# Positional query columns of four heads in one product, placed by DMA copies

## The chip, the cores and the metric

The kernel runs on one core of a Trainium2 chip. A core has a matrix engine (TensorE, in the profile PE, its weight loads PEld), a vector engine (VectorE, DVE), an activation engine (ScalarE, ACT), a general engine (GpSimd, POOL) and an engine that mostly issues transfers (SyncE, SP). Each follows its own list of instructions in order, and they wait for one another by semaphores. The metric is the device time of one execution in microseconds. Before the change it is 903.84, the median of three runs (903.61 to 907.07).

## The reference

The input x is 8 batches of 512 tokens with 128 features. A modulation row per batch (silu(c) @ Wmod) gives shifts, scales and gates. The block is an attention with relative positions and a mixture of experts:

```python
h = layernorm(x) * (1 + ca) + sa
q, k, v = einsum('bsx,xAnh->Abnsh', h, w)        # 16 heads of 64
q = q + q_bias
a = einsum('bnqh,bnkh->bnqk', q, k) * 64 ** -0.5
emb = einsum('sf,fnh->nsh', sins, positional)    # 32 frequencies
pos_scores = einsum('bnqh,nvh->bnqv', q, emb) * 64 ** -0.5
a = a + relative_causal(pos_scores)              # column = distance q - k
a = softmax(where(causal, a, -1e9))
x = x + ga * (concat_heads(a @ v) @ out_kernel + out_bias)
h = layernorm(x) * (1 + cb) + sb
x = x + gb * experts(h)                          # top 1 of 16, 256 places each
```

Since the sine of a difference of positions is a sum of products, the positional score of a query and a key at distance q - k is also a product of 64 numbers made from the query (32 frequencies, each times two tables over the query's position) with 64 numbers that depend on the key's position alone. So a head's score is one product over 128 numbers: 64 of content and 64 of position.

## The kernel before, in words

There are 64 attention steps: 8 batches (b), in each 8 pairs of heads (a), j = 8b + a. Steps of even and odd a use the two halves of several buffers. A query tile `qx` holds for each of the two heads 128 partitions: 0 to 63 the content of the query, 64 to 127 its positional numbers, by 512 queries. Both come out of one product a head: the weights `whi`/`wlo` of a pair have 128 columns for each head, 64 query columns and 64 columns of a positional weight (the query weight times the positional kernel, made once at the start by `w_table`, its 32 columns stored twice), and 128 columns for the keys of both heads. Products of activations and weights are done three times, with the high and low parts of either operand (`hi*hi`, `hi*lo`, `lo*hi`), so one product is three matmuls of 512 columns. VectorE adds the bias and multiplies by the table `qtab` as it evacuates the query (`evac_q`, L1106).

Within a step the engines go through eight score groups s0 to s7 (k = 0 to 7): first the four query tiles of the first head, from 512 keys down to 128, then those of the second head. For each k:

- TensorE: the scores (L773, L770) into one of two banks, then one group of transposes of the previous step's probabilities (L783, k = 0 to 5), at k = 1 a value product (L759), at k = 2 the output projection of two steps ago (L810), after s4 the next step's query product of the first head (L738), at k = 5 the next key product (L738), at k = 7 the weighted sum of the previous step (L803), and last the next query product of the second head (L738).
- VectorE: subtracts mask and negates with a running maximum (L1089), at k = 0 one transposed group (L1097) and the low part of the attention output (L1118), at k = 1 the low part of the second head's keys (`low_k`, L1112), at k = 4 the first head's query (L1106); at the end of the step `low_k` of the next step's first head, reciprocals and the second head's query. Layer norms, gating and routing are spread over fixed (a, k).
- ScalarE: exponentials (L553), the high part of the queries (L518), transposed groups (L562), values (L522), the high part of the keys (L512) and their copy `kx` (L513), the attention output (L567). At (a, k) = (2, 4) it normalizes the next batch (`normed`, L499), out of the bank that also takes the second head's query and the value product (`prb[1]`).
- GpSimd: the low part of the queries (L388) and the division of the probabilities (L395), modulation, and the indirect writes of tokens to the experts' buffer.
- SP: weights and stores; at the start of batch 0 the gates' rows go to all partitions, the experts' buffer is filled (4 transfers) and 8 expert weights are loaded.

The order is written out by hand in the Python loops; nothing plans it. After the 64 steps comes a tail with the last batch's routing, and then the 16 experts.

## Time and profile before

| | us |
|---|---|
| median of three runs | 903.84 |
| the profiled execution's own time | 906.07 |
| its span, first to last instruction | 904.0 |
| TensorE busy | 875.8 (97%) |
| ScalarE busy | 710.3 (79%) |
| VectorE busy | 665.9 (74%) |
| GpSimd busy | 518.7 (57%) |

An engine's busy time is the time in which an instruction of it is under way. A timeline row gives the start from the start of the span, the duration, engine, line of the source, operation and tiles (what is written, then what is read). Matmuls overlap: one of 512 columns is shown with 0.40 us, but the next one starts some 0.23 us later. The distance of starts is what TensorE's order costs. The mean granted clock of TensorE is 0.991 of full speed.

### The profile page before, as it was taken

Reading aid. Unit: us, or ns where it says so; the run is one execution under the profiler, and the core shown is the slowest. Engines: PE = TensorE matmul, PEld = TensorE weight load, DVE = VectorE, ACT = ScalarE, POOL = GpSimd, SP = SyncE. Lnnn points to the kernel's source line nnn. Section 1 sums busy time; section 2 is a strip of 40 time slices with the busy share of each in tenths; the row PEclk is TensorE's granted clock in tenths of the full one; section 3 lists DMA queues with packets and bytes.
Section 4 is the critical chain, followed back from the end, with each engine's and each line's share of the span. In section 5 each row is a group of like instructions: output and inputs, shape, how many; then the busy total and the mean of one; then the engine's idle time right before and its main releaser. Section 6 shows DMA issues by size and latency. Waiting matters only on the chain.

```text
span 904.0 us, 17653 instructions
## 1 busy us (share of the span) xinstructions
PE 875.8 (97%) x5632; PEld 702.2 (78%) x5632; DVE 665.9 (74%) x2053; ACT 710.3 (79%) x1970; POOL 518.7 (57%) x786
## 2 busy tenths in 40 slices
PE   6999999999999999999999999999999999997994
PEld 5777777887777778777777877777887777766994
DVE  4778778787878687777878787868777677753884
ACT  4788888888888888888888888888888888841551
POOL 2455555565565755675557556675566556633354
PEclk9899999999999999999999999999999999999998
DMA  7000790000000000000000000000000000006671
GB/s 271 2 1 1 190 243 24 1 19 18 13 1 2 36 1 13 1 28 10 13 1 15 12 13 1 2 21 8 5 1 22 2 13 1 9 22 218 215 213 39
DMA packets 23068, 38.92 MB, mean 43 GB/s; under 512 B 3094, under 2 KB 16135, under 8 KB 22592
## 3 DMA queue, kind: packets, MB, share of 16 engines
q1 hardware_dynamic: 19184, 29.11, 11.1%
q0 software_dynamic: 3072, 5.94, 1.8%
q10 hardware_dynamic: 720, 2.75, 0.9%
q8 instruction: 45, 0.74, 0.3%
q14 instruction: 47, 0.39, 0.1%
HBM read 23.44 MB, written 16.82 MB: 45 GB/s over the span
## 4 chain that ended last, share of the span: by engine, by line
PE 86%; DVE 1%; POOL 1%; DMA 1%; issue 1%; ACT 1%; POOLq 0%; DVEq 0%
PE bank L773 21%; PE bank L803 16%; PE bank L738 15%; PE bank L783 14%; PE bank L810 5%; PE bank L759 4%; PE bank L770 3%; PE bank L981 2%; PE bank L970 2%; DMA x<-xbuf 1%; PE bank L831 1%; POOL out L443 1%; PE bank L961 0%; PE bank L818 0%; PE bank L825 0%
## 5 line engine op out<-in xcount | busy, mean ns | idle before, releaser
L395 POOL TENSOR_SCALAR prob<-prob,rsum 128x128 f32<-128x128 f32 (+3 forms) x512 | 263.1, 532 | 238.4 <-DVE rsum L1101 232.4
L553 ACT ACTIVATE prob<-srow,nmax 128x512 f32<-128x512 f32 (+3 forms) x512 | 286.3, 560 | 66.5 <-DVE nmax L1089 63.7
L1089 DVE CUSTOM_DVE_ANT_0 srow<-bank,consts 128x512 f32<-128x512 f32 (+3 forms) x512 | 247.0, 488 | 98.0 <-issue 76.4
L783 PE MATMUL bank<-consts,prob 128*128 128x128 f32 x1280 | 201.7, 272 | 0.2 <-POOL prob L395 0.2
L783 PEld LDWEIGHTS bank<-consts,prob 128*128 128x128 f32 x1280 | 158.4, 140 | 22.9 <-POOL prob L395 0.5
L388 POOL TENSOR_TENSOR qlo<-qx,qhi 128x384 fp32r<-128x384 f32 x128 | 129.5, 1012 | 54.5 <-ACT qhi L518 53.2
L562 ACT ACTIVATE pt<-bank 128x384 f32<-128x384 f32 x318 | 153.3, 495 | 5.4 <-PE bank L783 5.0
L803 PE MATMUL bank<-pt,v 128*64 128x512 f32 (+3 forms) x1024 | 152.0, 439 | 0.3 <-issue 0.2
L773 PE MATMUL bank<-khi,qhi 128*128 128x512 f32 (+2 forms) x384 | 146.0, 380 | 3.5 <-DVE klo L1112 1.7
L1106 DVE SCALAR_TENSOR_TENSOR qx<-bank,qbias,consts 128x512 f32<-128x512 f32 x128 | 94.2, 736 | 53.6 <-PE bank L738 53.5
L773 PE MATMUL bank<-khi,qlo 128*128 128x512 f32 (+2 forms) x384 | 130.4, 339 | 0.0
L773 PE MATMUL bank<-klo,qhi 128*128 128x512 f32 (+2 forms) x384 | 129.5, 337 | 0.0
L803 PEld LDWEIGHTS bank<-pt,v 128*64 128x64 f32 x1024 | 68.1, 136 | 76.8 <-issue 59.3
L1112 DVE SCALAR_TENSOR_TENSOR klo<-bank,khi 64x512 fp32r<-64x512 f32 x128 | 87.8, 686 | 18.0 <-ACT kx L513 16.0
L553 ACT ACTIVATION_READ_ACCUMULATOR prob<-srow,nmax 128x1 f32 x512 | 97.8, 191 | 0.0
L518 ACT ACTIVATE qhi<-qx 128x384 fp32r<-128x384 f32 x128 | 66.6, 521 | 37.2 <-DVE qx L1106 36.5
L773 PEld LDWEIGHTS bank<-khi,qhi 128*128 128x128 f32 x384 | 72.6, 189 | 17.0 <-issue 7.9
L738 PE MATMUL bank<-hhi,whi 128*128 128x512 f32 x177 | 81.4, 460 | 0.0
L773 PEld LDWEIGHTS bank<-klo,qhi 128*128 128x128 f32 x384 | 73.1, 190 | 7.5
L512 ACT ACTIVATE khi<-bank 64x512 fp32r<-64x512 f32 x128 | 75.2, 588 | 3.7 <-PE bank L738 2.1
L773 PEld LDWEIGHTS bank<-khi,qlo 128*128 128x128 f32 x384 | 72.5, 189 | 5.5
L738 PE MATMUL bank<-hlo,whi 128*128 128x512 f32 x177 | 70.4, 398 | 0.0
(166 smaller groups left out, 1429.4 us busy)
## 6 DMA issues: line engine op xcount, KB each, us to landing
xbuf<-fill SPq DMA_DIRECT2D x4, 1540.0 KB, 24.4
x<-xbuf SPq DMA_DIRECT2D x16, 385.0 KB, 4.0
raw<-in_w SPq DMA_DIRECT2D x16, 256.0 KB, 8.9
prob<-in_w SPq DMA_DIRECT2D x16, 256.0 KB, 4.7
out<-row SPq DMA_DIRECT2D x8, 256.0 KB, 2.3
x<-in_x SPq DMA_DIRECT2D x1, 1792.0 KB, 13.2
modb<-mod_rows SPq DMA_DIRECT2D x1, 1536.0 KB, 7.8
v<-in_b SPq DMA_DIRECT2D x1, 1024.0 KB, 7.4
```

What stands on the lines that cost most here:

```text
L388: gp.tensor_tensor(qlo[:, h, :], qx[:, h, P:S], qhi[:, h, :], ALU.subtract).then_inc(s["ql"], 1)
L395: end = gp.tensor_scalar(part, part, rsum[:, par, 4 * h + q:4 * h + q + 1], 1.0, ALU.mult, ALU.mult)
L512: act.activation(khi[0:HD, h, :], prb[0][h * HD:(h + 1) * HD, :], ACT.Copy, scale=C_QKV)
L553: act.activation(prob[:, par, h, QOFF[q]:QOFF[q] + P * (q + 1)], srow[:, k % 4, 0:P * (q + 1)], ACT.Exp, bias=nmax[:, par, k:k + 1], scale ...
L562: act.activation(pt[:, h, KOFF[g]:KOFF[g] + GW[g]], source[:, 0:GW[g]], ACT.Copy)\
L738: last = pe.matmul(out, w[:, a, cols], h, start=(i == 0), stop=(i == 2))
L773: last = pe.matmul(out, a[:, h, (q - 1) * P:q * P], b[:, h, 0:P * (q + 1)], start=(i == 0), stop=(i == 2))
L783: last = pe.transpose(out[:, n * P:(n + 1) * P], prob[:, par, h, QOFF[q] + k * P:QOFF[q] + (k + 1) * P], ident)
L803: last = pe.matmul(otb[h * HD:(h + 1) * HD, k * P:S], v[:, g, k, at + h * HD:at + (h + 1) * HD], pt[:, h, KOFF[k]:KOFF[k] + S - k * P], st ...
L1089: dve.tensor_tensor_reduce(out=srow[:, k % 4, 0:w], in0=scb[k % 2][:, 0:w], in1=mask[:, S - w:S], scale=-1.0, scalar=BIG, op0=ALU.add, op1 ...
L1106: dve.scalar_tensor_tensor(qx[:, h, :], prb[h][:, :], qbias[:, h, a:a + 1], qtab, ALU.add, ALU.mult).then_inc(s["qe"], 1)
L1112: dve.scalar_tensor_tensor(klo[0:HD, h, :], prb[0][h * HD:(h + 1) * HD, :], C_QKV, khi[0:HD, h, :], ALU.mult, ALU.subtract).then_inc(s["kl ...
```

## The change

Queries: one product a step gives the 64 content columns of both heads (128 columns). It stands ahead of s3 now, in `prb[0]`, and waits until both `low_k` of the present step have read that bank. VectorE evacuates it by two tensor_scalar of 64 partitions, ahead of s3 and s4; the second head's moves from partitions 64 to 127 of the bank to partitions 0 to 63 of `qx`.

Positional numbers: in every even step, behind s6, one product gives the 32 raw frequency columns of four heads (the next pair of steps), in `prb[1]`. VectorE evacuates it twice (`evac_g`, at k = 6 and 7), once with each of the two tables (`gtab`), into `g2`. Four transfers on SP (`spread`) then copy the parts into partitions 64 to 127 of `qx`. `qx` has two halves by the step's parity.

The value product at k = 1 waits for `evac_g` or for the tail uses of its bank. SP's order: each step's copies come first; the fill is cut into 16 transfers over the steps of batch 0, expert weights are loaded over batch 1, and the gates' rows, for two batches at a time, ahead of their use. The first step's query is still done by two products with their own weights (`fwhi`, `fwlo`), which GpSimd then copies for later batches. The weight splits are fewer and wider.

```diff
@@ SP
+            def spread(j):
+                c, odd = divmod(j, 2)
+                wait(sp, "sc", 8 * (j - 1) if j > 1 else 0)
+                sp.wait_ge(s["gq"], 2 * c + 2)
+                for h in range(2):
+                    at = odd * CH + h * FREQS
+                    for i in range(2):
+                        sp.dma_start(qx[HD + i * FREQS:HD + (i + 1) * FREQS, odd, h, :], g2[at:at + FREQS, i, :])\
+                            .then_inc(s[f"gx{odd}"], 16)
...
@@ ScalarE
             def high_q(j, h):
                 act.wait_ge(s["qe"], 2 * j + h + 1)
-                act.activation(qhi[:, h, :], qx[:, h, P:S], ACT.Copy).then_inc(s["qh"], 1)
+                wait(act, f"gx{j % 2}", 64 * ((j + 1) // 2))
+                act.activation(qhi[:, h, :], qraw(j, h)[:, P:S], ACT.Copy).then_inc(s["qh"], 1)
...
@@ TensorE
+            def project_q(j, n, a):
+                pe.wait_ge(s["kl"], 2 * j)
+                project(prb[0][:, :], whi[:, a, 0:P], wlo[:, a, 0:P], n, "qp")
+            def project_g(c):
+                project(prb[1][:, :], gwhi[:, c % NG, :], gwlo[:, c % NG, :], g_batch(c), "tp")
...
                 for k in range(8):
+                    if k == 3 and after:
...
+                        project_q(j + 1, n, m)
                     scores(j, k)
-                    if k == 4 and after:
-                        project_q(j + 1, n, m, 0)
...
                     if k == 5 and after:
...
+                        pe.wait_ge(s["qe"], 2 * j + 4)
                         project_k(j + 1, n, m)
...
+                    if k == 6 and a % 2 == 0 and j + 2 < NJ:
+                        pe.wait_ge(s["ve"], j + 4 if before else 1)
+                        if a == 2 and not last:
+                            pe.wait_ge(s["hn"], b + 2)
+                        if a == 4 and not first:
+                            pe.wait_ge(s["lge"], b)
+                        project_g(j // 2 + 1)
...
-                    project_q(j + 1, n, m, 1, 8 * B if last and V_OF[a][0] else j + 4 if before else 2)
...
@@ VectorE
             def evac_q(j, a, h):
-                dve.wait_ge(s["qp"], 2 * j + h + 1)
-                dve.scalar_tensor_tensor(qx[:, h, :], prb[h][:, :], qbias[:, h, a:a + 1], qtab,
-                                         ALU.add, ALU.mult).then_inc(s["qe"], 1)
+                dve.wait_ge(s["qp"], j + 2)
+                own = slice(h * HD, (h + 1) * HD)
+                dve.tensor_scalar(qraw(j, h)[0:HD, :], prb[0][own, :], pbias[own, a:a + 1], CQ, ALU.add, ALU.mult)\
+                    .then_inc(s["qe"], 1)
+            def evac_g(c, i):
+                dve.wait_ge(s["tp"], c + 1)
+                if c:
+                    dve.wait_ge(s["gx1"], 64 * c)
+                    wait(dve, "gx0", 64 * (c - 1))
+                dve.scalar_tensor_tensor(g2[:, i, :], prb[1][:, :], gbias[:, c % NG:c % NG + 1], gtab[:, i, :],
+                                         ALU.add, ALU.mult).then_inc(s["gq"], 1)
...
                 for k in range(8):
+                    if k in (3, 4) and after:
+                        evac_q(j + 1, (a + 1) % PAIRS, k - 3)
                     scores(j, par, k)
...
-                        if after:
-                            evac_q(j + 1, (a + 1) % PAIRS, 0)
+                    if k in (6, 7) and a % 2 == 0 and j + 2 < NJ:
+                        evac_g(j // 2 + 1, k - 6)
...
-                if after:
-                    evac_q(j + 1, (a + 1) % PAIRS, 1)
```

## Rows read from the trace of the kernel before

**Rows 1.** The page: busy time of the engines, and the chain by engine.
```profile
PE 875.8 (97%) x5632; PEld 702.2 (78%) x5632; DVE 665.9 (74%) x2053; ACT 710.3 (79%) x1970; POOL 518.7 (57%) x786
...
PE 86%; DVE 1%; POOL 1%; DMA 1%; issue 1%; ACT 1%; POOLq 0%; DVEq 0%
```
**Rows 2.** Timeline (start, duration, engine, line, names), TensorE, step (4,6) and after.
```profile
486.96 0.40 PE L773 MATMUL bank<-khi,qhi 128*128 128x512 f32 x1
...
491.04 0.38 PE L770 MATMUL bank<-kx,qx 128*128 128x128 f32 x2
...
492.43 0.40 PE L738 MATMUL bank<-hhi,whi 128*128 128x512 f32 x1
...
493.13 0.49 PE L783 MATMUL bank<-consts,prob 128*128 128x128 f32 x3
...
497.99 0.50 PE L738 MATMUL bank<-hhi,whi 128*128 128x512 f32 x1
...
498.79 0.39 PE L773 MATMUL bank<-khi,qhi 128*128 128x512 f32 x1
```
**Rows 3.** Timeline, TensorE, the first step's bias products.
```profile
23.23 1.36 PE L694 MATMUL bank<-smallT,raw 128*32 128x1 f32 x56
```
**Rows 4.** Timeline, VectorE, step (4,6).
```profile
487.95 0.69 DVE L1089 CUSTOM_DVE_ANT_0 srow<-bank,consts 128x512 f32<-128x512 f32 x1
...
490.36 0.69 DVE L1112 SCALAR_TENSOR_TENSOR klo<-bank,khi 64x512 fp32r<-64x512 f32 x1
491.08 0.42 DVE L1089 CUSTOM_DVE_ANT_0 srow<-bank,consts 128x256 f32<-128x256 f32 x1
...
492.73 0.69 DVE L1089 CUSTOM_DVE_ANT_0 srow<-bank,consts 128x512 f32<-128x512 f32 x1 [0.87 <-issue]
...
496.71 0.68 DVE L1112 SCALAR_TENSOR_TENSOR klo<-bank,khi 64x512 fp32r<-64x512 f32 x1 [0.40 <-ACT kx L513]
```
**Rows 5.** Groups by line and shape, VectorE: busy us, mean ns, idle before.
```profile
L1358 DVE TENSOR_SCALAR srow<-bank,smallT 128x256 f32<-128x256 f32 x32 | 15.2, 481 | 3.1 <-PE bank L970 2.5
...
L1128 DVE TENSOR_SCALAR hn<-bank,bo,modT 128x512 f32<-128x512 f32 x8 | 6.5, 807 | 1.2 <-PE bank L810 1.2
```
**Rows 6.** Timeline, a wait that ends: VectorE's maximum releases TensorE.
```profile
39.68 0.08 DVE L1089 DVE_READ_ACCUMULATOR2_ANT nmax<- 128x1 f32 x1
...
39.82 0.49 PE L770 MATMUL bank<-kx,qx 128*128 128x128 f32 x2 [0.67 <-DVE nmax L1089]
```
**Rows 7.** Timeline, ScalarE, step (4,6): the copy of the next keys.
```profile
496.41 0.26 ACT L513 ACTIVATE kx<-bank 64x128 f32<-64x128 f32 x1
```
**Rows 8.** Timeline, TensorE, step (4,3): transposes of the second norm.
```profile
457.14 0.60 PE L825 MATMUL bank<-consts,xh 128*128 128x128 f32 x4
```
**Rows 9.** Timeline, ScalarE and TensorE, step (4,2): the normalization, and s7.
```profile
445.23 0.77 ACT L499 ACTIVATE hn<-bank,modT 128x512 f32<-128x512 f32 x1
...
446.36 0.39 PE L770 MATMUL bank<-kx,qx 128*128 128x128 f32 x2
```
**Rows 10.** Timeline, VectorE and TensorE, step (4,4), its s0 and the next one's.
```profile
462.07 0.39 PE L773 MATMUL bank<-khi,qhi 128*128 128x512 f32 x1
...
471.65 0.42 DVE L1089 CUSTOM_DVE_ANT_0 srow<-bank,consts 128x256 f32<-128x256 f32 x1 [0.15 <-ACT prob L553]
...
473.98 0.67 DVE L1112 SCALAR_TENSOR_TENSOR klo<-bank,khi 64x512 fp32r<-64x512 f32 x1
...
474.79 0.44 PE L773 MATMUL bank<-khi,qhi 128*128 128x512 f32 x1
```
**Rows 11.** Timeline, VectorE, step (4,5): s5 and the klo at its end.
```profile
482.44 0.56 DVE L1089 CUSTOM_DVE_ANT_0 srow<-bank,consts 128x384 f32<-128x384 f32 x1 [0.42 <-issue]
...
486.12 0.68 DVE L1112 SCALAR_TENSOR_TENSOR klo<-bank,khi 64x512 fp32r<-64x512 f32 x1
```
**Rows 12.** The page, transfers: count, KB each, median us from issue to landing.
```profile
out<-row SPq DMA_DIRECT2D x8, 256.0 KB, 2.3
```

More of the change, by code:

```diff
@@ new lines, in gate_rows @@
+            def gate_rows(p):
+                wait(sp, "h2", p - 1)
+                wait(sp, "gg", p - 1)
+                sp.dma_start(modb[:, p % 2, :, :].rearrange("p a d -> p (a d)"),
+                             mod_dram[p:p + 1, :].to_broadcast([P, 3 * D])).then_inc(s[f"modb{p % 2}"], 16)
+            def turn(b, first, last):
+                for a in range(PAIRS):
+                    j = 8 * b + a
+                    if j:
+                        spread(j)
+                    if first and a:
+                        for i in range(2 * a - 2, 2 * a):
+                            clear(i)
+                    if (b, a) == (1, 0):
+                        for i in (14, 15):
+                            clear(i)
+                        sp.wait_ge(s["gates"], 2)
+                        sp.dma_start(mod_dram, mrow[:, :, :].rearrange("p a d -> p (a d)")).then_inc(s["mrow"], 16)
+                    if (b, a) == (1, 1):
+                        sp.wait_ge(s["mrow"], 16)
+                        gate_rows(0)
+                        gate_rows(1)
+                        sp.wait_ge(s["flo"], 3)
+                        sp.wait_ge(s["qwl"], 2)
+                        sp.wait_ge(s["kwl"], 2)
+                        sp.wait_ge(s["wv"], 2)
+                        sp.wait_ge(s["wg_mm"], 6)
+                    if b == 1 and a:
+                        load_w1(a - 1, a - 1)
+                    if a == 3 and not first:
+                        store(b)
+                        if b > 1:
+                            gate_rows(b)
+                    if (b, a) == (2, 0):
+                        load_w1(7, 7)
@@ L769, in scores @@
                 if q == 0:
-                    last = pe.matmul(out, qx[:, h, 0:P], kx[:, h, :], start=True, stop=True)
+                    last = pe.matmul(out, qraw(j, h)[:, 0:P], kx[:, h, :], start=True, stop=True)
                 else:
@@ L912, in step @@
                         pe.wait_ge(s["mev"], 1)
-                        pe.wait_ge(s["bias"], 3)
                     if k == 7 and before:
                         weighted(j - 1, (a - 1) % PAIRS, 8 * b + 4 * ((a - 1) // 4) + 4)
-                if after:
-                    if a == 2 and not last:
-                        pe.wait_ge(s["hn"], b + 2)
-                    if a in (1, 3, 4, 5) and not first:
-                        pe.wait_ge(s[("x2", None, "hh", "lge", "prx")[a - 1]], b)
-                    project_q(j + 1, n, m, 1, 8 * B if last and V_OF[a][0] else j + 4 if before else 2)
             pe.wait_ge(s["fhi"], 3)
             pe.wait_ge(s["flo"], 3)
-            project_q(0, None, 0, 0)
-            project_q(0, None, 0, 1)
+            pe.wait_ge(s["vlo"], 1)
+            for h in range(2):
+                project(prb[h][:, :], fwhi[:, h, :], fwlo[:, h, :], None, "qp")
             pe.wait_ge(s["wall1"], 16)
             w_table(1, 4)
+            b_table(0, 4)
+            pe.wait_ge(s["qe"], 1)
             project_k(0, None, 0)
@@ L1308, in first_step @@
                     low_wv()
-                if k == 4:
-                    dve.wait_ge(s["bias"], 3)
+                if k in (2, 3):
+                    evac_g(0, k - 2)
                 if k == 5:
-                    low_g(4, PAIRS, "whi", 5, "wlo")
+                    low_g(1)
             def rows_of():
@@ L1322, in _ @@
             dve.wait_ge(s["bias"], 2)
-            evac_q(0, 0, 0)
-            evac_q(0, 0, 1)
-            for h in range(2):
-                low_wq(1, 4, h, h + 1)
+            first_q(0)
+            first_q(1)
+            low_wq(1, 4, 1)
             low_k(0, 0)
-            low_g(1, 4, "whi", 4, "wlo")
+            low_g(0)
+            dve.wait_ge(s["pbias"], 1)
+            dve.wait_ge(s["gtab"], 16)
+            dve.wait_ge(s["bias"], 3)
             batches(turn)
@@ L1439 @@
     arrays, args = {}, []
[L1440 removed]
+    consts, ktab, gtab = host_constants()
     laid = layouts({n: np.asarray(a) for n, a in inputs.items()})
[L1442 removed]
+    for name, a in laid + [("consts", consts), ("ktab", ktab), ("gtab", gtab)]:
         a = np.ascontiguousarray(a)
```

295 lines of the change are left out of this document (155 added, 140 removed), and 1 row of the table names.

## The prediction

> **What bounds the kernel now.** I read the page's busy shares first, then its chain of waits: TensorE is busy 97% of the span and 86% of the chain that ended last is TensorE [rows 1]. So a product taken away is worth its place in TensorE's order, as long as no other engine holds up what follows. The timeline of one attention step then shows who follows how closely. I name a step by batch and head pair, (4,6), and its eight score groups s0 to s7. Step (4,6) has nothing but the eight-fold pattern in it and takes 486.96 to 498.79, 11.83 us [rows 2]; in it TensorE never stands, though VectorE and ScalarE come close behind, and that closeness is the whole question.
>
> **What goes and what comes on TensorE.** Query products of 3 matmuls go from two a step to one, and one positional product comes in every even step. Of the old ones, 63 (the second head's) go; 32 come; 31 net. One costs 0.70 (492.43 to 493.13); the one that goes took 0.80 (497.99 to 498.79) because it came first behind the weighted sum, and that 0.10 passes on to s0 [rows 2]. Gain: 31 x 0.70 = 21.7 us, or 2.8 in a batch (8 go, 4 come). In the first step 56 bias products of 1.36 us become 8, with 8 more before it, and the tables are half as wide [rows 3]; the first positional product, counted above, stands there too. I take 1 us for the start, between 0 and 2.
>
> **What comes on VectorE.** Before: two evacuations of 128x512 a step. After: two tensor_scalar of 64x512 from PSUM each step, and two of 128x512 in even steps. Half the rows aren't half the time: the 64x512 klo row takes 0.68 to 0.69 [rows 4], and a tensor_scalar of 256 columns from PSUM already takes 0.481 where the bounds for 512 are that and 0.807 [rows 5]. I take 0.75, which is 0.63 from start to start where the next one overlaps it. So 0.63 a step more on average, 1.3 in even steps. The odd head's evacuation reads partitions 64 to 127 and writes 0 to 63, as the odd head's klo does; that one starts 0.04 behind its predecessor's end and the next starts only at its own end, 490.36 to 491.08 = 0.72 for a 0.69 instruction [rows 4]. I charge the new one 0.25 over 0.63 for both sides (bounds 0 and 0.25).
> The Trainium skill, "VectorE: DVE Perf Modes", section "Two Vector instructions with no wait between them", says that an instruction whose operand starts in another quadrant than the last one's waits for all earlier ones to finish; by it the new evacuation is held and holds its successor, which speaks against the change; without it the sum would be 6 us lower.
>
> **Where the cover is gone.** Times below count from s0 of a step. A consumer of another engine starts 0.06 after the producer's end in one wait of the trace (39.76 to 39.82) [rows 6]; I take 0.10.
>
> *Every step, before the query product.* It moves from behind s4 to ahead of s3, and waits for the odd head's klo, since it overwrites that bank. TensorE comes there at 4.08 + 0.10 = 4.18 (491.04 is 4.08) [rows 2]. VectorE starts s0 at 0.99 before, 1.09 now, and ends klo 3.10 later (487.95 to 491.05) [rows 4]: 4.19, and 4.29 on TensorE. With a weight load no longer hidden (0.08, as in the 0.80 against 0.70) I take 0.19; bounds 0 and 0.3. 62 steps: 12 us. Everything behind it on TensorE moves with it.
>
> *Odd plain step (a=7).* TensorE would reach the next s0 at 11.83 + 0.10 + 0.19 - 0.80 = 11.32. But s4 now comes behind the query product and behind both query evacuations on VectorE: the product stands at 4.37, lasts 0.70 with a tail of 0.2 (a 0.40 row at a spacing near 0.23), so q0 starts at 5.30; 0.63 for it, 0.36 for s3 and its maximum, 0.75 for q1 (held) make 7.04, and s4 starts at 7.07 where it was 492.73, 5.77. ScalarE has no pause from its exponential of s4 to the next keys: kx ends 496.67, 3.94 behind s4 [rows 4, 7]. So kx ends 11.01, klo 11.71, TensorE 11.81: 0.49 late. Queued behind are all of the next step's products.
>
> *a=1 and a=3.* VectorE has residual (0.807 [rows 5], 0.75 from start to start) or two normalizations (about 0.5) between s3 and s4; TensorE has transposes (0.60 as a row, about 0.45 in the order) [rows 8]. 0.49 + 0.75 - 0.45 = 0.8 and 0.5.
>
> *a=2.* The positional product overwrites the bank that ScalarE normalizes from (L499), so it waits for it. That row ends 446.00, and the product's new place is where s7 started, 446.36 [rows 9]: 0.36 of slack, and 0.65 since TensorE comes 0.10 + 0.19 later. But s4 on VectorE, and this row behind it, moves by 1.52 (by the 1.30 of the plain step and by two statistics ahead of q1, about 0.3). 1.52 - 0.65 + 0.10 = 1.0 late (bounds 0.4 and 1.1) in batches 1 to 6, and 0.65 in batch 0, where the statistics are missing.
>
> *a=4.* From s6 to the end of klo VectorE is busy 471.65 to 474.65 = 3.00, full, and TensorE took klo at 474.79 [rows 10]: no slack. In it go the two positional evacuations, 2 x 0.63, and 0.25 of waiting for their product. s6 starts at 9.58 + 0.10 + 0.19 = 9.87; klo ends 14.38, TensorE 14.48. TensorE's own sum is 474.79 - 462.07 = 12.72, + 0.10 + 0.19 - 0.80 + 0.70 = 12.91. 1.6 late, in batches 1 to 6; 1.0 in batch 7 (no vlo there), 0.4 in batch 0 (no gating).
>
> *a=5.* From s5 to the end of klo VectorE has 4.36 us of work, 482.44 to 486.80 (placement, routing) [rows 11], and s0 came at 486.96 [rows 2], 12.17 into the step. s5 still comes with TensorE's order (+0.29), TensorE's end comes 0.51 earlier (-0.80 + 0.29): 12.01 + 0.29 + 0.10 against 11.66, 0.75 late.
>
> *a=0, a=6.* The positional product gives back the 0.70. Its evacuations start at 9.62, 10.46 behind s7, and klo ends 11.8; TensorE needs it at 11.32 + 0.70 = 12.02. Nothing, with 0.1 to spare.
>
> *Hidden.* ScalarE's work is the same; GpSimd's too but two copies in batch 0. The copies that place the columns: four on SP a step, behind the last score of two steps ago. A 256 KB transfer lands 2.3 us after issue [rows 12]. evac_g ends some 0.6 ahead of the next step, and ScalarE wants the columns 9.6 into it; even four such transfers of 64 KB one after another (9.2) would fit. Clears, gates' rows and expert loads stand behind them in SP's order, one or two a step.
>
> **Sum.** A batch of 1 to 6: -2.8 + 1.5 (8 x 0.19) + 0.8 + 1.0 + 0.5 + 1.6 + 0.75 + 0.5 = +3.85, six times 23.1. Batch 0: -2.1 + 1.3 + 0.5 + 0.65 + 0.5 + 0.4 + 0.5 + 0.5 = +2.2 (5 positional products). Batch 7: -2.8 + 1.3 + 0.8 + 0.5 + 1.0 + 0.75 = +1.6. Start: -1. Together +26 us on the profiled execution's own 906.07 (span 904.0), which lies 2.2 above the median of 903.84; on the median: 929 us.
>
> **Rivals.**
> *A, faster.* The same gain and no waits: 903.84 - 22.7 = 881. The mechanism is slack on VectorE: if its row ends at klo, s4 and vlo come earlier than I place them. All waits together are 49 us; 0.19 earlier takes the 12 of the query product and 0.19 from each of some 46 others, leaving +5; from 0.3 earlier the sum is zero, from 0.4 it is 0.5% faster. For it: VectorE is busy 74% of the span [rows 1], and a 64-row evacuation could be 0.48. Against: its start times are tied to TensorE's, so that share helps only between them, and nothing shortens klo's 3.10.
> *B, the waits half as long.* -22.7 + 24 = +2: 900 to 910. For it: each is a difference of two sums some 10 long.
> *C, the columns late.* If the four copies land 1 us after ScalarE wants them in each step, that is 60 us more, 960 and up. It decides from 10 us between evac_g and the landing. Against: the 2.3 us of a transfer four times as large [rows 12].
> *D, the change doesn't cut TensorE's work*, since padding takes it back: the counts of products exclude it.
>
> **How the numbers follow.** Forecast 0.72 (own range 912 to 940), A 0.12, B 0.11, C 0.05; D nothing. Faster by over 0.5% (about what a measurement tells from no change): A and 0.01 of B, 0.13. Within 0.5%: 0.08, of B. Slower: 0.72 + 0.05 + 0.02 = 0.79. The range starts at 900, where B starts, and ends at 940, the forecast's own end with the upper bounds of the first wait; A and C lie outside with 0.17.
>
> **What would show it.** L738's successor should have 31 x 3 matmuls fewer. TensorE should have idle time now, under 50 us in all, on: the query product, released by klo; the positional product in a=2, released by ScalarE's hn; and s0 behind a=4 and a=5, released by klo. The steps of one batch should be unequal, a=4 about 14.5 us, a=6 12.0, a=7 11.8. VectorE's evacuation of 64x512 should take 0.7 to 0.8. If steps a=0 and a=6 grow too, I missed a cost; if a=7 takes 11.1, rival A is right; if ScalarE's qhi waits for a DMA, C is.

## The result

The changed kernel takes 934.3 us, median of four runs (933.27 to 935.22); the kernel before took 905.5 beside it (903.61 to 908.2). The ratio is 1.032, with a 95% interval of 1.028 to 1.035: slower by 3.2%. The forecast was 929, range 900 to 940.

Two lines of the changed kernel's page answer to [rows 1]: busy time and instructions of the engines, and the chain of waits by engine.

```profile
PE 869.1 (93%) x5515; PEld 684.8 (73%) x5515; DVE 702.9 (75%) x2115; ACT 704.5 (76%) x1971; POOL 519.2 (56%) x789
...
PE 87%; issue 5%; DVE 2%; ACT 2%; DMA 1%; POOL 1%; SPq 0%; DVEq 0%; POOLq 0%; ACTq 0%
```

TensorE has 117 matmuls fewer, of which 93 are the 31 products of the forecast. Its share of the span fell from 97% to 93%: it now stands idle where it never did, and "issue" in the chain grew from 1% to 5%. VectorE has 37 us more work, yet its share went only from 74% to 75%. So the loss is not in any engine's total; it must be looked for in the order.

The distance from one s0 to the next, read from TensorE's timeline, shows where. In batches 1 to 6 these lengths repeat within some 0.05 us, but for a few single steps (of which the last paragraph tells). All kernels of this study stand here, since every experiment is read from this table (us, the typical length of each step in batches 1 to 6, and the sum of the eight):

| kernel | a=0 | 1 | 2 | 3 | 4 | 5 | 6 | 7 | sum |
|---|---|---|---|---|---|---|---|---|---|
| before | 11.94 | 12.28 | 12.27 | 12.28 | 12.72 | 12.18 | 11.83 | 11.83 | 97.3 |
| changed, forecast | 12.13 | 12.57 | 13.47 | 12.27 | 14.5 | 12.42 | 12.03 | 11.82 | 101.2 |
| changed, measured | 12.15 | 12.47 | 13.47 | 12.31 | 14.22 | 12.36 | 11.98 | 11.78 | 100.7 |
| control: kernel before, keys first | 11.94 | 12.27 | 12.26 | 12.27 | 12.72 | 12.13 | 11.83 | 11.84 | 97.3 |
| product behind s3 | 12.10 | 12.45 | 13.42 | 12.26 | 14.06 | 12.19 | 11.73 | 11.60 | 99.8 |
| narrow positional evacuation | 12.15 | 12.48 | 13.47 | 12.30 | 13.69 | 12.36 | 11.97 | 11.79 | 100.2 |
| norm first | 12.15 | 12.48 | 12.88 | 12.30 | 14.22 | 12.37 | 11.97 | 11.79 | 100.2 |
| no copies | 12.15 | 12.48 | 13.47 | 12.30 | 14.22 | 12.37 | 11.97 | 11.79 | 100.8 |
| both from the same partitions | 12.01 | 12.22 | 13.33 | 12.05 | 14.06 | 12.14 | 11.97 | 11.55 | 99.3 |
| keys first | 12.16 | 12.47 | 13.47 | 12.29 | 12.96 | 11.81 | 12.66 | 11.79 | 99.6 |
| three reorderings | 12.11 | 12.31 | 12.83 | 12.27 | 12.80 | 11.61 | 12.38 | 11.61 | 97.9 |
| and high part first | 12.07 | 12.61 | 12.83 | 12.21 | 12.65 | 11.54 | 12.02 | 11.55 | 97.5 |
| queries behind s4 alone | 11.82 | 11.58 | 12.32 | 11.58 | 13.99 | 12.49 | 11.78 | 11.55 | 97.1 |
| queries behind s4, ends redone | 11.81 | 11.72 | 12.32 | 11.56 | 12.71 | 12.40 | 11.78 | 11.56 | 95.9 |
| and placement behind s7 | 11.81 | 11.72 | 12.32 | 11.56 | 12.71 | 11.65 | 11.81 | 11.56 | 95.1 |

The next fence is the changed kernel's timeline of step (3,6), the same kind of step as that of [rows 2, 4]: TensorE's s0, query product and next s0, VectorE's klo, the two query evacuations, s4, the first positional evacuation and the last klo, and ScalarE's copy of the keys.

```profile
404.63 0.47 PE L837 MATMUL bank<-khi,qhi 128*128 128x512 f32 x1 [0.62 <-issue]
...
408.84 0.50 PE L804 MATMUL bank<-hhi,whi 128*128 128x512 f32 x1
...
416.60 0.50 PE L837 MATMUL bank<-khi,qhi 128*128 128x512 f32 x1
...
408.10 0.69 DVE L1207 SCALAR_TENSOR_TENSOR klo<-bank,khi 64x512 fp32r<-64x512 f32 x1
...
409.84 0.74 DVE L1192 TENSOR_SCALAR qx<-bank,pbias 64x512 f32<-64x512 f32 x1 [0.59 <-PE bank L804]
...
410.82 0.76 DVE L1192 TENSOR_SCALAR qx<-bank,pbias 64x512 f32<-64x512 f32 x1
411.61 0.69 DVE L1168 CUSTOM_DVE_ANT_0 srow<-bank,consts 128x512 f32<-128x512 f32 x1
...
414.19 0.75 DVE L1201 SCALAR_TENSOR_TENSOR g<-bank,gbias,gtab 128x512 f32<-128x512 f32 x1 [0.17 <-PE bank L804]
...
415.72 0.67 DVE L1207 SCALAR_TENSOR_TENSOR klo<-bank,khi 64x512 fp32r<-64x512 f32 x1
...
415.30 0.27 ACT L573 ACTIVATE kx<-bank 64x128 f32<-64x128 f32 x1
```

The query product starts 4.21 into the step, 0.05 behind klo's end (408.10 + 0.69), and VectorE starts s4 at 6.98 where it was 5.77 [rows 4]. In a=6 that has room: the weighted sum keeps TensorE busy until the next s0.

In the plain odd step it hasn't. Next is the end of (3,7), which begins at 416.60: ScalarE's last two transposed groups, which stand behind the exponential of s4; TensorE's weighted sum, which reads them, and the next s0; VectorE's klo.

```profile
425.08 0.85 ACT L620 ACTIVATE pt<-bank 128x384 f32<-128x384 f32 x2
...
426.03 2.37 PE L867 MATMUL bank<-pt,v 128*64 128x512 f32 x16 [0.34 <-issue]
428.39 0.47 PE L837 MATMUL bank<-khi,qhi 128*128 128x512 f32 x1
...
427.61 0.68 DVE L1207 SCALAR_TENSOR_TENSOR klo<-bank,khi 64x512 fp32r<-64x512 f32 x1 [1.37 <-ACT kx L573]
```

TensorE's idle time stands ahead of the weighted sum here, which starts 0.10 behind the last transposed group (425.93). From there to the next s0 it is 2.36; in a=6, where neither of the two waits, it is 2.30. klo ends at 428.29, 0.10 ahead of that s0. So two chains hang on the late s4, one through the transposed group and the weighted sum, one through the keys and klo, and they end within 0.06 of each other. In the whole kernel the weighted sum waits 25 times, 10.8 us in all.

In a=4 there is no room either. The end of (3,4): VectorE's first positional evacuation, the small operation behind it, then the second one, the low part of the norm, klo; TensorE's next s0 comes with klo, after 1.35 us of idleness. The last two rows are ScalarE's norm in (3,2) and the positional product that waited for it.

```profile
388.41 0.75 DVE L1201 SCALAR_TENSOR_TENSOR g<-bank,gbias,gtab 128x512 f32<-128x512 f32 x1
389.07 0.48 DVE L1267 SCALAR_TENSOR_TENSOR lgt<-lgt,consts 128x64 f32<-128x64 f32 x1
...
390.21 0.75 DVE L1201 SCALAR_TENSOR_TENSOR g<-bank,gbias,gtab 128x512 f32<-128x512 f32 x1
390.87 0.68 DVE L1121 TENSOR_TENSOR vlo<-hn,vhi 128x512 fp32r<-128x512 f32 x1
391.47 0.68 DVE L1207 SCALAR_TENSOR_TENSOR klo<-bank,khi 64x512 fp32r<-64x512 f32 x1
...
392.25 0.47 PE L837 MATMUL bank<-khi,qhi 128*128 128x512 f32 x1 [1.35 <-issue]
...
361.46 0.77 ACT L559 ACTIVATE hn<-bank,modT 128x512 f32<-128x512 f32 x1
...
362.33 0.47 PE L804 MATMUL bank<-hhi,gwhi 128*128 128x512 f32 x1 [0.88 <-issue]
```

### The profile page after: what moved, and what is told of

Read it like the earlier page. It is cut to its first block, busy times and chain, and to the rows that moved or that the text cites. A ratio compares the mean times of both kernels' runs of the same rounds, so it can differ in the third digit from the quotient of the medians.

```text
span 932.6 us, 18151 instructions
## 1 busy us (share of the span) xinstructions
PE 869.1 (93%) x5515; PEld 684.8 (73%) x5515; DVE 702.9 (75%) x2115; ACT 704.5 (76%) x1971; POOL 519.2 (56%) x789
## 4 chain that ended last, share of the span: by engine, by line
PE 87%; issue 5%; DVE 2%; ACT 2%; DMA 1%; POOL 1%; SPq 0%; DVEq 0%; POOLq 0%; ACTq 0%
PE bank L837 23%; PE bank L867 15%; PE bank L847 15%; PE bank L804 13%; PE bank L823 5%; PE bank L874 4%; PE bank L834 3%; PE bank L1059 2%; PE bank L1048 2%; PE bank L1012 2%; ACT prob L611 1%; DMA kx<-in_ktab 1%; PE bank L895 1%; DVE klo L1207 1%; DMA x<-xbuf 1%
## 5 line engine op out<-in xcount | busy, mean ns | idle before, releaser
L847 PE MATMUL bank<-consts,prob 128*128 128x128 f32 x1280 | 204.2, 274 | 0.2 <-POOL prob L451 0.2
L847 PEld LDWEIGHTS bank<-consts,prob 128*128 128x128 f32 x1280 | 155.1, 141 | 28.2 <-ACT pt L620 7.5
L837 PE MATMUL bank<-khi,qhi 128*128 128x512 f32 (+2 forms) x384 | 151.7, 395 | 18.8 <-issue 16.3
L867 PE MATMUL bank<-pt,v 128*64 128x512 f32 (+3 forms) x1024 | 151.9, 438 | 12.8 <-issue 10.8
L867 PEld LDWEIGHTS bank<-pt,v 128*64 128x64 f32 x1024 | 76.0, 136 | 84.0 <-issue 64.3
L1192 DVE TENSOR_SCALAR qx<-bank,pbias 64x512 f32<-64x512 f32 x126 | 94.4, 749 | 26.9 <-PE bank L804 24.3
L804 PE MATMUL bank<-hhi,whi 128*128 128x512 f32 x118 | 57.4, 487 | 0.9 <-DVE klo L1207 0.9
L1201 DVE SCALAR_TENSOR_TENSOR g<-bank,gbias,gtab 128x512 f32<-128x512 f32 x64 | 47.9, 749 | 11.9 <-PE bank L804 11.7
```

Of the source, the lines that this page charges most:

```text
L804: last = pe.matmul(out, w, h, start=(i == 0), stop=(i == 2))
L837: last = pe.matmul(out, a[:, h, (q - 1) * P:q * P], b[:, h, 0:P * (q + 1)], start=(i == 0), stop=(i == 2))
L847: last = pe.transpose(out[:, n * P:(n + 1) * P], prob[:, par, h, QOFF[q] + k * P:QOFF[q] + (k + 1) * P], ident)
L867: last = pe.matmul(otb[h * HD:(h + 1) * HD, k * P:S], v[:, g, k, at + h * HD:at + (h + 1) * HD], pt[:, h, KOFF[k]:KOFF[k] + S - k * P], st ...
L1192: dve.tensor_scalar(qraw(j, h)[0:HD, :], prb[0][own, :], pbias[own, a:a + 1], CQ, ALU.add, ALU.mult)\
```

## Experiments

Times are medians, ratios are to the kernel before run beside it, with their 95% intervals. The diffs are against the changed kernel.

**1. The query product behind s3.**

```diff
-                    if k == 3 and after: ... project_q(j + 1, n, m)
                     scores(j, k)
+                    if k == 3 and after: ... project_q(j + 1, n, m)
```

On VectorE both evac_q go between s3 and s4.

> The query product stands behind s3 instead of ahead of it, and VectorE evacuates both halves between s3 and s4. Theory (the product waits for the odd head's klo, which ends just as TensorE arrives): s3's 0.22 us now cover the wait, so each step loses the 0.19 that it waited, and s4 starts about 0.2 earlier on VectorE against the step, which a=1, 2, 3 and 7 need. Steps a=0 and 6 become 11.95 and 11.8, a=7 11.6, a=2 13.25, a=4 14.0; in all 12 to 14 us less, about 921. Rival (the loss is VectorE's added load as a whole, and the wait only shows it): the same work stands on VectorE, so steps stay within 0.05 and the time at 934.

Measured: 928.1 us, ratio 1.025 (1.020 to 1.029). The product no longer waits for klo, but that gives 6 us and not 12. By the table, a = 4 to 7 gain 0.16 to 0.25 each, a = 0 to 3 only 0.02 to 0.05. VectorE shows why. Its s4 comes some 0.16 earlier in (3,4) to (3,7), 6.82 into (3,4) where it was 6.98; in (3,0), (3,2) and (3,3) only 0.03 to 0.05 (7.34 where it was 7.39 in (3,0)), since there the pieces of a layer norm stand ahead of s4 too and fill VectorE from the first evacuation to s4. In (3,1) s4 gains 0.17, but klo then starts 0.18 behind its keys, behind the second residual. The edit also takes s3's maximum from between the two evacuations, so it isn't the wait alone that it removes.

**2. A narrow positional evacuation.** From the second product on, evac_g covers one column of 512.

```diff
-                dve.scalar_tensor_tensor(g2[:, i, :], prb[1][:, :], ...
+                w = 1 if c else S
+                dve.scalar_tensor_tensor(g2[:, i, 0:w], prb[1][:, 0:w], ...
```

> From the second positional product on, VectorE evacuates one column of the 512 (the result is left incomplete), so that the two positional evacuations cost some 0.15 instead of 0.66 from start to start each. Theory (they matter in a=4 alone, where klo stands behind them and nothing else covers): a=4 falls from 14.22 to about 13.2, a=0, 2 and 6 stay within 0.1; in all 6 to 8 us less, about 927. Rival (VectorE's total load): every even step falls by 0.5 to 1.0, over 20 us less, 914 or below.

Measured: 929.0 us, ratio 1.025 (1.020 to 1.029). In the repeated batches only a=4 moved, by 0.53; in batch 0 a=4 went from 13.86 to 12.69. In a = 0, 2 and 6 the same work is gone from VectorE, and those steps stay the same to 0.01. So evac_g counts in a=4 alone, as forecast, and VectorE's total isn't the limit. The gain is smaller than the 1.06 taken away (the next instruction starts 0.13 behind a narrow one, 0.66 behind a full one, twice), and the timeline of a=4 in this kernel shows where the rest went: the small operation behind the evacuation now takes 1.00 us, where it took 0.48.

```profile
384.44 0.22 DVE L1202 SCALAR_TENSOR_TENSOR g<-bank,gbias,gtab 128x1 f32<-128x1 f32 x1
384.57 1.00 DVE L1268 SCALAR_TENSOR_TENSOR lgt<-lgt,consts 128x64 f32<-128x64 f32 x1
...
384.50 1.00 POOL L444 TENSOR_TENSOR qlo<-qx,qhi 128x384 fp32r<-128x384 f32 x1 [0.43 <-ACT qhi L579]
```

It reads two tiles of SBUF, and it ends 0.07 behind GpSimd's low part of the queries (385.57 against 385.50), which began just ahead of it. More on this at the end.

**3. ScalarE's norm ahead of the exponential of s4 in a=2.**

```diff
+                    if k == 4 and a == 2 and not last:
+                        normed(b + 1)
                     exps(j, par, k)
```

> ScalarE normalizes the next batch ahead of the exponential of s4 instead of behind it and a transposed group. Theory (in a=2 the positional product waits for it): the product starts where TensorE gets to it, a=2 falls from 13.47 to about 12.6, other steps unchanged; 6 us less, about 928. Rival (a=2 is long because of the two statistics on VectorE): a=2 stays above 13.3.

Measured: 931.5 us, ratio 1.027 (1.023 to 1.032). a=2 falls from 13.47 to 12.88, nothing else moves. The forecast's mechanism for a=2 holds: the positional product was late because ScalarE's hn stood behind s4. The 0.28 that is missing went into another wait. In this kernel's (3,3) s0 waits for GpSimd, which could not begin its division before VectorE's reciprocals behind s4:

```profile
359.49 2.07 POOL L451 TENSOR_SCALAR prob<-prob,rsum 128x128 f32<-128x128 f32 x4 [4.88 <-DVE rsum L1180]
...
364.02 0.50 PE L837 MATMUL bank<-khi,qhi 128*128 128x512 f32 x1 [0.47 <-POOL qlo L444]
```

**4. Without the copies.** From batch 1 on `spread` is left out, with the waits on it.

```diff
-                    if j:
+                    if 0 < j < 8:
                         spread(j)
```

> From batch 1 on, the transfers that place the positional columns are left out (the columns of batch 0 stay). Theory (they land long before they are wanted, and cost nothing): all steps of batches 1 to 7 within 0.05 of before, time within 1 us of 934; only single long steps, as a=4 of batch 4 at 14.59 and a=7 of batch 6 at 12.14, could go. Rival (transfers late or in the way of other traffic): 5 us or more less.

Measured: 934.9 us, ratio 1.032 (1.027 to 1.037), and every step of batches 1 to 6 is the same to 0.02. Rival C falls: the copies cost nothing. The page gives them as `qx<-g`, 252 of 64 KB, 2.0 us to landing, and ScalarE's qhi waits for no DMA.

**5. Both heads' evacuations from the same partitions.**

```diff
-                own = slice(h * HD, (h + 1) * HD)
+                own = slice(0, HD)
```

> The odd head's query evacuation reads partitions 0 to 63 of the bank like the even head's (so its content columns are the wrong head's); nothing else is changed. My theory charged this instruction 0.25 us for reading another quadrant than its neighbours and holding them: s4 behind it comes 0.1 to 0.25 earlier, and with it klo in the steps that end on VectorE's chain (a = 1, 3, 4, 5, 7): each 0.1 to 0.25 shorter, a = 0 and 6 unchanged, -4 to -8 us in all (926 to 930). Rival: the two neighbours wait for the product and for the exponential anyway, so the hold costs nothing: every step within 0.03 of the changed kernel, 934.

Measured: 924.9 us, ratio 1.019 (1.016 to 1.022). That is 9 us, a little more than expected (4 to 8). The timeline of (3,6) in this kernel, to be set beside the one above:

```profile
405.80 0.74 DVE L1192 TENSOR_SCALAR qx<-bank,pbias 64x512 f32<-64x512 f32 x1 [0.58 <-PE bank L804]
...
406.67 0.74 DVE L1192 TENSOR_SCALAR qx<-bank,pbias 64x512 f32<-64x512 f32 x1
407.33 0.67 DVE L1168 CUSTOM_DVE_ANT_0 srow<-bank,consts 128x512 f32<-128x512 f32 x1
```

From the first evacuation to s4 it is 1.53, in the changed kernel 1.77 (409.84 to 411.61). The durations are the same; the starts are 0.11 and 0.13 closer. The forecast charged 0.25 for both sides, measured is 0.24. By the table a = 1, 3 and 7 each lose 0.23 to 0.26, a=5 0.22, a=2 and a=4 some 0.15, a=6 nothing: the steps that end on VectorE's chain, as forecast. a=0 loses 0.14, which the forecast had without a wait. The rule of the Trainium skill cited in the forecast ("VectorE: DVE Perf Modes", section "Two Vector instructions with no wait between them") agrees with this trace: in the changed kernel s4 starts 0.03 behind the end of the second evacuation (411.58), here 0.08 ahead of it (407.41). The edit moved the partitions of the bank and of the bias together, so it doesn't say which of the two holds.

**6. Keys first.** Nothing is removed; in a = 1, 4 and 5 VectorE's klo comes ahead of residual2, of the second evac_g and `low`, and of routing and index.

```diff
                 if after:
                     low_k(j + 1, 0)
+                if a == 1 and not first: residual2(b)
+                if a == 4: evac_g(j // 2 + 1, 1); low(b + 1)
                 recip(j, par, 1)
+                if a == 5 and not first: route(b); index(b)
```

> VectorE computes the next step's first klo ahead of what can wait: in a = 1 ahead of the second residual, in a = 4 ahead of the second positional evacuation and of the low part of the norm, in a = 5 ahead of routing and index; no work is added or taken away. My theory: in a = 4 and 5 the next s0 waits for klo behind these. a = 4 from 14.22 to about 13.1 (0.63 and 0.69 no longer ahead of it, less what is then late in the next step), a = 5 from 12.36 to 11.8, a = 1 from 12.47 to 12.3: -1.8 a batch, -12 to -14 us in all, 921. Rival: klo's own input (ScalarE's kx behind its exponentials) is what comes late, then a = 4 falls by under 0.3 and a = 5 by nothing: 932.

Measured: 925.4 us, ratio 1.021 (1.017 to 1.025), not the 921 expected. a=4 went to 12.96 and a=5 to 11.81 as expected; a=1 didn't move, since klo starts 0.03 behind its keys there before and after: residual2 had not been in its way. But a=6 rose from 11.98 to 12.66. In this kernel the reciprocals wait for the last exponential of a=5, routing and index stand behind them, and s0 of a=6 starts on VectorE 1.75 into the step where it is 1.06 in the changed kernel. More than a third of the gain (0.68 of 1.81 a batch) was given back one step later.

**7. The three reorderings together** (1, 3 and 6), and **8.** with ScalarE's high part of the queries ahead of the exponential of s4.

> Three reorderings together, none of which adds or takes away work: the query product behind s3, ScalarE's norm ahead of the exponential of s4 in a = 2, klo first in a = 1, 4 and 5. If each wait is its own, their gains add: 6 (measured alone) + 3 (measured alone) + 13 (expected alone) = 22, 912. Steps in batches 1 to 6 near 12.1, 12.3, 12.8, 12.2, 13.0, 11.6, 11.7, 11.6. Rival: they are links of one chain through VectorE and ScalarE, which closes again behind each: then half, 922 to 925.

> The kernel with the three reorderings, and in addition ScalarE makes the high part of the next step's first queries ahead of the exponential of s4 instead of behind it, in the hole in which it waits for s4. My theory: a = 7 (and 1, 3, 5) end on the chain s4, exponential, keys, klo, which has no pause on ScalarE; one evacuation of 0.5 us less behind s4 shortens each odd step by 0.3 to 0.5: -10 to -14 us against x7_all, near 900. Rival: ScalarE isn't what ends the odd steps, or its hole ahead of s4 is too short and delays s4's exponential as much: within 3 us of x7_all.

Measured: 913.3 us, ratio 1.007 (1.0045 to 1.010), and 911.4 us, ratio 1.007 (1.004 to 1.010). The gains add. The 22 us expected counted "keys first" with the 13 expected of it; with the 9 that it gave, the three alone are 18, and together they give 21. Part of the surplus is a=1, where klo first pays once s4 is earlier (12.45 to 12.31).

The eighth gave some 2 us in the median and not 10: a=7 moved from 11.61 to 11.55 and a=1 got longer by 0.3. The end of (3,7), which begins at 405.26, shows that klo's chain was not alone. ScalarE's transposed groups, TensorE's weighted sum and next s0, VectorE's klo:

```profile
413.55 0.85 ACT L620 ACTIVATE pt<-bank 128x384 f32<-128x384 f32 x2
...
414.50 2.38 PE L868 MATMUL bank<-pt,v 128*64 128x512 f32 x16 [0.42 <-issue]
416.80 0.50 PE L838 MATMUL bank<-khi,qhi 128*128 128x512 f32 x1
...
415.66 0.68 DVE L1208 SCALAR_TENSOR_TENSOR klo<-bank,khi 64x512 fp32r<-64x512 f32 x1 [1.03 <-ACT kx L573]
```

klo ends 0.46 ahead of s0 now, so the keys came earlier as the theory said. But the weighted sum still waits 0.42 for the transposed group behind the exponential of s4, and it ends the step. Both chains begin at VectorE's s4, which stands behind both evacuations at 6.83 into this step (5.77 before the change). That led to the next one.

**9. The queries behind s4, as before the change.** This kernel keeps the change and redoes its order: on TensorE the query product behind s4 and the key product behind s6, on VectorE both evac_q behind s4, klo ahead of both evac_g, and most of 6 (routing stays ahead of klo). ScalarE's first high part of the queries comes ahead of the exponential of s5; its norm stays where the changed kernel has it. The load of the positional tables comes later, and in a = 2 and 4 the positional product stands behind the key product.

```diff
 TensorE
-                    if k == 3 and after: ... project_q(j + 1, n, m)
                     scores(j, k)
+                    if k == 4 and after: ... project_q(j + 1, n, m)
-                    if k == 5 and after: ... project_k(j + 1, n, m)
+                    if k == 6 and after: ... project_k(j + 1, n, m)
 VectorE
-                    if k in (3, 4) and after:
-                        evac_q(j + 1, (a + 1) % PAIRS, k - 3)
                     scores(j, par, k)
                     if k == 4:
                         recip(j, par, 0)
+                        if after: evac_q(.., 0); evac_q(.., 1)
 ScalarE
+                    if after and k == 5: high_q(j + 1, 0)
                     exps(j, par, k)
```

> The change kept, its order redone: the query product and both of its evacuations behind s4 (as in the kernel before), so that s4's maximum no longer waits for them; the key product behind s6, where TensorE has the time; the positional product ahead of it in a = 0 and 6, behind it in 2 and 4; VectorE's klo ahead of both positional evacuations, of the second residual, of the low part of the norm and of the index; ScalarE's high part of the queries ahead of the exponential of s5; the load of the positional tables behind the keys' table. My theory (the loss is where the pieces were put, not what they cost): TensorE ends an odd plain step near 11.4 and an even one near 12.0; a = 0 to 7 about 12.1, 11.9, 12.4, 11.9, 12.4, 11.6, 12.0, 11.4 = 95.7 a batch against 97.3 before: 888 to 896, below both kernels. Rival: VectorE's added 1.3 us a step pair is itself what binds, wherever it stands: then the klo of each step is late again and the time stays near the 911 to 913 of the reordered kernels.

Measured: 897.9 us, ratio 0.992 (0.990 to 0.995): faster than both kernels, by 0.8% than the kernel before, and just outside the 888 to 896 expected. Seven steps of a batch are within 0.35 of what was expected; a=5 is 12.40 and not 11.6. Its end in the timeline, VectorE, GpSimd and TensorE:

```profile
479.44 1.02 DVE L1292 TENSOR_TENSOR lgt<-lgt,oh 128x64 f32<-128x64 f32 x1
...
481.71 0.16 DVE L1299 SCALAR_TENSOR_TENSOR rsm<-rsm 128x4 f32<-128x4 f32 x1
481.91 0.68 DVE L1214 SCALAR_TENSOR_TENSOR klo<-bank,khi 64x512 fp32r<-64x512 f32 x1
...
479.39 1.00 POOL L445 TENSOR_TENSOR qlo<-qx,qhi 128x384 fp32r<-128x384 f32 x1
...
482.69 0.47 PE L839 MATMUL bank<-khi,qhi 128*128 128x512 f32 x1 [0.68 <-issue]
```

The placement's small product of two SBUF tiles takes 1.02 instead of 0.23, again ending 0.07 behind GpSimd's qlo, and klo stands behind it and routing.

**10. A control: klo first in the kernel before** (ahead of `low` in a=4, of the index in a=5).

> Control, the kernel before with the same kind of reordering: klo ahead of the low part of the norm in a = 4 and of the index in a = 5. Its a = 4 takes 12.72 where its TensorE work is some 12.3, a = 5 12.18 where it is 11.9. My theory: klo is the last to come there too, a = 4 becomes 12.3 and a = 5 11.95, less some 0.1 given back in the next step: -4 us, 900. Rival: TensorE's own order binds these steps: within 1 us of 903.84.

Measured: 903.8 us, ratio 0.999 (0.998 to 1.001). Here the theory was wrong. a=4 stays at 12.72: what ends it is TensorE's own work, and moving VectorE's queue has nothing to give. The record goes further than this one control. In batches 1 to 6 of the kernel before, TensorE is busy in 583.88 us of 583.88; in the changed kernel it is busy in 578.37 of 605.13, and in the best version below in 569.79 of 571.84. Where TensorE never stands, a new order of the other engines has next to nothing to give. So the gains above aren't ones that the kernel before would have had as well; they undo what the change cost.

**11. The placement behind s7, routing and index behind klo and the reciprocals**, added to 9 (the load of the positional tables goes back to its old place).

> The redone order (897.9) with one more stretch moved: in a = 5 VectorE's placement behind s7 instead of s5, routing and index behind the next klo and the reciprocals; the table load back in its old place. In the redone order a = 5 takes 12.40, TensorE's own work ends there at 11.64, and s0 waits 0.68 for a klo that starts behind routing. Theory: a = 5 becomes 11.7 to 11.9, a = 6 at most 0.2 longer, the rest unchanged: -0.5 a batch, 7 batches, 893 to 896. Rival: the placement delays klo as much from its new place: 897 to 899.

Measured: 893.3 us, ratio 0.986 (0.984 to 0.989). a=5 is 11.65, and a=6 rose by 0.03 only. This is the best version: 12 us faster than the kernel before, with the change in it. Its busy line, and the product that took 1.02 above, now beside an idle GpSimd:

```profile
PE 860.7 (97%) x5515; PEld 688.0 (77%) x5515; DVE 698.2 (78%) x2115; ACT 708.3 (79%) x1971; POOL 519.3 (58%) x789
...
478.35 0.23 DVE L1291 TENSOR_TENSOR lgt<-lgt,oh 128x64 f32<-128x64 f32 x1
```

**12. The queries behind s4 alone.** Only TensorE's and VectorE's part of the diff of 9; the ends of the steps stay as in the changed kernel.

> The changed kernel with one thing moved: the query product and both of its evacuations behind s4 (TensorE and VectorE), the key product with them behind s6. The ends of the steps (evac_g, klo, gating, routing) and ScalarE's order stay as in the changed kernel. The chain that I forecast (query product waits for klo 0.19; s4 behind both evacuations, +1.3 on ScalarE's keys) is gone from every step. If it was the cause in the odd plain steps, a = 7 falls from 11.8 to 11.6, a = 1 and 3 from 12.5 and 12.3 to 11.9, a = 2 from 13.47 to 12.9; a = 4 and 5 keep VectorE's queue ahead of klo (13.5, 12.2): 915. If the ends of the steps are what counts, the gain is only the 6 us that the product behind s3 gave: 928.

Measured: 905.9 us, ratio 1.0005 (0.999 to 1.002). This one move is worth 28 us, 9 of them more than the theory gave it. a = 1, 3 and 7 are at 11.55 to 11.58, a=2 at 12.32, all without a change on ScalarE; a=4 and a=5 keep their queue ahead of klo, at 13.99 and 12.49 (expected 13.5 and 12.2). No weighted sum of these steps waits any more, and klo ends 0.36 ahead of the next s0 in (3,7): both chains from s4 are gone. VectorE in (3,6), to be read against the first timeline:

```profile
396.60 0.69 DVE L1173 CUSTOM_DVE_ANT_0 srow<-bank,consts 128x512 f32<-128x512 f32 x1 [0.90 <-issue]
...
397.31 1.51 DVE L1197 TENSOR_SCALAR qx<-bank,pbias 64x512 f32<-64x512 f32 x2
398.85 0.56 DVE L1173 CUSTOM_DVE_ANT_0 srow<-bank,consts 128x384 f32<-128x384 f32 x1
```

s0 stood at 390.77, so s4 starts 5.83 in, as before the change (5.77), and the two evacuations fill time in which VectorE had waited. What is left in the odd steps is the key product, which waits for the second evacuation. TensorE in (3,7):

```profile
410.25 0.28 PE L837 MATMUL bank<-khi,qlo 128*128 128x256 f32 x1
410.69 0.50 PE L804 MATMUL bank<-hhi,whi 128*128 128x512 f32 x1 [0.16 <-DVE qx L1197]
411.02 0.39 PE L804 MATMUL bank<-hlo,whi 128*128 128x512 f32 x1
```

The row shows 0.16 of idle time, but by the starts the wait costs more: the product starts 0.44 behind a matmul of 256 columns, where the distance is otherwise 0.12, and its second matmul 0.33 behind its first, where 0.23 is usual. That is 0.4 us, the whole distance from TensorE's own sum without waits (11.83 + 0.10 - 0.80 = 11.13, the forecast's terms) to the 11.55 measured.

## Why the forecast was right, and where it was not

The sign, the size and the places came as forecast, and of eight step lengths the largest error is 0.28. Part of the total is luck, since errors cancel. The profiled execution is 28.6 us longer than the one before, forecast were 26. Batches 1 to 6 give 21.3 of it (forecast 23.1), batch 0 4.1 (2.2), batch 7 2.4 (1.6) and the start 0.8 (-1).

*The gain.* 31 products went. In the best version a batch is 2.2 us shorter than before; the forecast set 2.8. Most of the rest is the key product's wait of experiment 12. It can't be seen in the changed kernel itself, since waits cover it.

*Query product behind klo, 12 us.* The mechanism is there (product at 4.21, klo's end at 4.16), but it isn't worth 12 us by itself. Taken away alone it returns 6 us, and in a = 0 to 3 next to nothing, since VectorE is full ahead of s4 there (experiment 1). The lengths of these steps still came out, for they are set by s4.

*Odd steps: s4 behind both evacuations.* a=7 11.78 against 11.82, a=3 12.31 against 12.27, a=1 12.47 against 12.57. Shown by experiment 12, in which s4 goes back and a = 1, 3 and 7 fall to 11.55 to 11.58. The hold of 0.25 in it was 0.24. The forecast had one of two ways from s4 to the next s0: klo's. The other, the transposed group behind the exponential of s4 and the weighted sum, was missed. It ends at almost the same time, so the length came out; that is luck, and it is why experiment 8 failed.

*a=2, waiting for hn.* 13.47, as forecast, and shown by experiment 3. That GpSimd's division is nearly as late was missed.

*a=4, klo behind two evac_g.* 14.22 against 14.5. Cause shown twice (2 and 6); the size was too large by 0.3, since klo ended 14.13 into the step and not 14.38.

*a=5.* 12.36 against 12.42; experiment 6 shows that it was the queue ahead of klo.

*a=0 and 6, nothing.* a=6 11.98 against 12.03, a=0 12.15 against 12.13, and untouched by the width of evac_g. In a=0 the reason was off: klo ended 12.06 into (3,0) and not 11.8, because the statistics of a layer norm put s4 at 7.39 there and not near 7.0. It released s0, close to when TensorE's own work would have.

*Batch 0 and the start.* Forecast +2.2 and -1, measured +4.1 and +0.8. In a=4 of batch 0 s0 came some 1.7 late (13.86, against TensorE's sum of 12.16) and not 0.4: with one-column evacuations the step falls by 1.2, so evac_g is in it again. Something else is too: a modulation's operation on 8x128 numbers from SBUF stands between the two evacuations, and takes 1.12 where it takes 0.28 in experiment 2's kernel (rows below, the changed kernel first). It lies beside GpSimd's qlo, as the last section tells.

```profile
87.27 1.12 DVE L1310 SCALAR_TENSOR_TENSOR xh<-xh,mrow 8x128 f32<-8x128 f32 x1
...
87.24 1.00 POOL L444 TENSOR_TENSOR qlo<-qx,qhi 128x384 fp32r<-128x384 f32 x1 [0.44 <-ACT qhi L579]
```

```profile
85.06 0.28 DVE L1311 SCALAR_TENSOR_TENSOR xh<-xh,mrow 8x128 f32<-8x128 f32 x1
```

In batch 7 a wait came where the forecast had none: in a=2 s0 comes 0.06 behind GpSimd's qlo, and the step takes 12.89 (11.94 before). What is left of batch 0 and the start can't be told apart, for this reason: step (0,0) took 13.69 in the kernel before and 11.51 in the control, whose instructions are the same up to there. The rows of granted clock in three windows, of the kernel before and then of the control (window, its length, TensorE busy, clock, DMA share, GB/s):

```profile
21.90:28.00 6.10, 6.10 (x77) 0.65 0.01 3
```

```profile
21.90:28.00 6.10, 5.45 (x81) 1.00 0.01 3
```

At a clock of 0.65 of full speed, part of that stretch ran at the lower of the two levels, and a matmul of 512 columns shows 0.63 us there and not 0.40. Terms of 1 us in the first 30 us are below what one profile can tell.

*The rivals.* A and B fall: the waits are there in nearly their forecast size. C falls by experiment 4, D by the count of matmuls. The forecast took the order as given. What it could have said from the trace of the kernel before is that VectorE stands idle 0.87 us ahead of s4 and 0.82 us ahead of s6, and that two evacuations of 0.75 fit behind s4 where they don't fit ahead of it.

## What to carry to other kernels

When a change adds work to an engine that has spare time, cost it by place: the same product and its two evacuations cost 28 us more ahead of the score on which a chain through two engines hangs than behind it. What the next step needs first goes ahead of all that can wait, and what is moved behind it is charged to the step after, since it may be given back there. A wait that stands in every step is worth only what the steps have that end on it, here half. And before one chain behind a late result is shortened, look whether a second one ends with it.

## What was not expected of the hardware

A VectorE operation that reads two tiles in SBUF can take four times its time while GpSimd works. The product of 64 columns takes 0.23 us beside an idle GpSimd and 1.02 beside qlo; three such operations (0.48, 1.00 and 1.02) each ended 0.07 to 0.08 behind the end of GpSimd's `qlo<-qx,qhi`, which takes 1.00. They do so in every batch in which they stand there, and the kernel before has a case as well (0.73 in place of 0.22, `oh<-lgt,rsm`). The evacuations, which read PSUM and at most one tile of SBUF, went on at their own time beside it: the first positional one in the fence of (3,4), 388.41, lies almost wholly beside qlo and takes its usual 0.75. Two tiles aren't always needed: the layer norm's `xn<-x,mom,rstd`, which reads one tile and two numbers a partition, takes 0.34 in the median and up to 1.10 beside GpSimd in the best version. The Trainium skill ("GPSIMD Engine Reference", section "Specifications") says that VectorE instructions with two SBUF inputs contend with GpSimd for its SBUF interfaces; these traces agree. It is why less work on VectorE in experiment 2 returned less than its own time: it brought the small operation under qlo's whole length.

In two steps of the changed kernel, (4,4) and (6,7), the length is 0.37 longer than in the other batches, and so it is in the best version in other steps, such as (3,2). In (4,4) the delay begins on VectorE, with the maximum of s0. The first row is that of (3,4), the second that of (4,4):

```profile
379.09 0.69 DVE L1168 CUSTOM_DVE_ANT_0 srow<-bank,consts 128x512 f32<-128x512 f32 x1
...
480.21 0.69 DVE L1168 CUSTOM_DVE_ANT_0 srow<-bank,consts 128x512 f32<-128x512 f32 x1 [0.50 <-PE bank L837]
```

They start 1.07 and 1.44 behind s0, though TensorE's s0 and VectorE's instruction ahead of them lie at the same distances. GpSimd's division and qlo follow late, by the same 0.37. It is not the copies, which experiment 4 left out without changing it. Its cause stays open.
